# Attention: first scores of four heads as one block behind the output product, in other PSUM banks

## The chip, the cores and the metric

The kernel runs on one core of a Trainium2 chip. The time is device microseconds of one execution. TensorE (PE) multiplies into PSUM, eight banks of 128 partitions by 512 fp32; VectorE (DVE) and ScalarE (ACT) read PSUM and work element by element; GpSimd (POOL) does so on SBUF only; SyncE (SP) issues DMAs. Each engine runs its own list of instructions in order and waits for the others by semaphores.

## What is computed

A stream of 4096 tokens (16 sequences of 256) with 256 features passes six layers: experts, attention, experts, a feed-forward with looked-up weights, a recurrent layer, and the same feed-forward again. The change is in the attention, which has 16 heads and 64 memory slots a head. Its reference, cut:

```python
def _chunk_abc(q, k, v, s):
    z = cumlogsumexp(s, axis=2)
    g = exp(concatenate([z[:, :, :1], z[:, :, :-1]], axis=2) - z)
    p = exp(s - z)
    def step_k(hk, x):                       # over time
        hk = hk * g_t[:, :, None, :] + k_t[..., None] * p_t[:, :, None, :]
        return (hk, einsum('bhk,bhkm->bhm', q_t, hk))
    pvT = softmax(okT, axis=-1)
    def step_v(hv, x):
        hv = hv * g_t[..., None] + p_t[..., None] * v_t[:, :, None, :]
        return (hv, einsum('bhm,bhmv->bhv', pv_t, hv))
s = clip(x @ Ws, -32, 32)
o = o * rsqrt(mean(square(o)) + EPS) * g_norm_weight
o = o * (g * sigmoid(g))
x = x + o.reshape(b, t, VALUE_DIM) @ Wo
```

## The kernel before

The stages run one behind the other, each in a block of its own; attention is one. It treats the recurrences as two causal products. With e = exp(clipped s), the first scores of a head are k against q over the 64 key features, masked so that only earlier times count; they are then applied to e (the slots' read), divided by the running sum of e, and put through a softmax over the 64 slots. The second scores are e turned against those weights over the 64 slots, masked likewise, and applied to v (the value read). Then come the norm, the gate and the output product.

A group is four heads of one sequence: N = 64 groups in order, index n, four to a sequence. Each of the 64 rounds of the loop works on the group n (slots' read, softmax, second scores, value read), on the group n + 1 (its projections and first scores) and on the group n - 1 (its turned output and output product). Every engine's order is written out by hand, and semaphores are counted by group.

PSUM is full: psA (two banks) takes the projections, psB (two banks) the scores, psC[0] turned and read things and the output product, psC[1] the turned exponentials and the turned read, psD (two banks) the value read of both time tiles and the turned output; psO names the two halves of psD.

A head's scores are two matmuls, 64 rows deep: times 0 to 127 against all 256, and times 128 to 255 against themselves, 384 columns in one bank (`causal_scores`, L1264). Even heads use partitions 0 to 63 of their operands, odd heads 64 to 127. In the trace each fp32 matmul leaves two records, and the projections and the output product are split into a high and a low part, three matmuls each (L1449 to L1451).

On TensorE a round ends: `over_j(n)` (the value read, L1323), `scores_a(n + 1)` for heads 0 and 1, `output(n - 1)` (L1344), `scores_a(n + 1)` for heads 2 and 3. The next begins with a value projection and the slots' read (L1294). Heads 2 and 3 of the first scores take the same psB banks as heads 0 and 1, so they wait for the masks of those (`at_ok`, L1280). The second scores (`scores_b`, L1283) use psB and both halves of psD.

On VectorE (L1142 on) the round ends: two gated outputs (L1109), masks of heads 0 and 1 (L1096), two gates (L1103), the output's addition `add_output(n - 1)` (L1083), masks of heads 2 and 3, and `squares(n)` (L1122). ScalarE squares the value read and takes the tanh of the gates. GpSimd turns the mean squares into a scale (L966) and scales the output (L971). In one period of four the next sequence is turned too (L1198).

Of the kernel before, what the change touches and what calls it, by code (L numbers as in the profile page):

```python
# [801 lines left out]
def attention(nc, cst, w, tag, past, stream_a, stream_b, x_out, second, zero_row, indices, looked_up):  # L802
# [10 lines left out]
    with ExitStack() as ctx:  # L813
# [38 lines left out]
        psO = [psD[:, k, :] for k in range(2)]  # L852

# [21 lines left out]
        with nc.Block(no_gpsimd_drain=True) as block:  # L875
# [180 lines left out]
            def _(dve):  # L1056
# [39 lines left out]
                def masked(n, heads, ps_ready, done, late=psB):  # L1096
                    for h in heads:
                        dve.wait_ge(ps_ready, HQ * n + h + 1)
                        bank = psB[h] if h < 2 else late[h - 2]
                        nc.vector.tensor_tensor(out=at[:, h, :], in0=bank[:, 0:3 * P],  # L1100
                                                in1=cst["causal"][:, :, :].rearrange("p a i -> p (a i)"), op=ALU.mult).then_inc(done, 1)
# [36 lines left out]
                masked(0, (0, 1), at_ps, at_ok)  # L1138
                gate(0, 0)
                gate(0, 1)  # L1140
                masked(0, (2, 3), at_ps, at_ok)
                for n in range(N):  # L1142
# [25 lines left out]
                    masked(n, range(HQ), bt_ps, bt_ok, psO)  # L1168
# [13 lines left out]
                    if ahead:  # L1182
                        masked(n + 1, (0, 1), at_ps, at_ok)
# [4 lines left out]
                    if ahead:  # L1188
                        masked(n + 1, (2, 3), at_ps, at_ok)
# [5 lines left out]
            def _(pe):  # L1195
# [68 lines left out]
                def causal_scores(lhs, rhs, h, ready, late=psB):  # L1264

                    a, r = h // 2, (h % 2) * DK
                    bank = psB[h] if h < 2 else late[h - 2]
# [4 lines left out]
                def scores_a(m, heads):  # L1272
                    for h in heads:
                        if h < 2:
                            if m > 0:
                                pe.wait_ge(bt_ok, HQ * m - 1 + h)
                            pe.wait_ge(k_ok, m + 1)
                            pe.wait_ge(q_ok, m + 1)
                        else:
                            pe.wait_ge(at_ok, HQ * m + h - 1)  # L1280
                        causal_scores(kT, qT, h, at_ps)

                def scores_b(n):  # L1283

                    pe.wait_ge(pzt_ok, n + 1)
                    pe.wait_ge(et_ok, n + 1)
                    for h in range(HQ):
                        if h < 2:
                            pe.wait_ge(at_ok, HQ * n + h + 3)
                        elif n > 0:  # L1290
                            pe.wait_ge(otl_ok, NH * n)
                        causal_scores(emT, pzT, h, bt_ps, psO)
# [68 lines left out]
                scores_a(0, (0, 1))  # L1361
                gate(0, 1)
                scores_a(0, (2, 3))
                for n in range(N):
# [24 lines left out]
                    if ahead:  # L1389
                        scores_a(n + 1, (0, 1))  # L1390
# [678 lines left out]
```

## Time and profile before

| | us |
|---|---|
| median of 3 runs | 2752.42 |
| lowest, highest | 2749.83, 2756.99 |
| the profiled execution | 2760.54 |
| its span | 2758.7 |
| PE, DVE, ACT, POOL busy in it | 2413.2, 1805.3, 864.9, 1245.1 |

The rows below come from the profiled execution, in us from the start of its span; the rest of its 2760.54 us lies around the span. The granted clock of TensorE is given as a share: 1.00 is 2.4 GHz, half of it 1.2 GHz. Matmuls are pipelined: a matmul's length in a row covers the start of the next, so the rate is to be read from the distance of the starts. In names, a_ stands for the attention stage; a_at holds masked scores.

### The profile page before, as it was taken

Reading aid. Unit: us, or ns where it says so; the run is one execution under the profiler, and the core shown is the slowest. Engines: PE = TensorE matmul, PEld = TensorE weight load, DVE = VectorE, ACT = ScalarE, POOL = GpSimd, SP = SyncE. Lnnn points to the kernel's source line nnn. Section 1 sums busy time; section 2 is a strip of 40 time slices with the busy share of each in tenths; the row PEclk is TensorE's granted clock in tenths of the full one; section 3 lists DMA queues with packets and bytes.
Section 4 is the critical chain, followed back from the end, with each engine's and each line's share of the span. In section 5 each row is a group of like instructions: output and inputs, shape, how many; then the busy total and the mean of one; then the engine's idle time right before and its main releaser. Section 6 shows DMA issues by size and latency. Waiting matters only on the chain. (4 is left out here: it accounts for less than half of the span.)

```text
span 2758.7 us, 44491 instructions
## 1 busy us (share of the span) xinstructions
PE 2413.2 (87%) x16926; PEld 2123.4 (77%) x16926; DVE 1805.3 (65%) x3578; ACT 864.9 (31%) x1704; POOL 1245.1 (45%) x1214
## 2 busy tenths in 40 slices
PE   6555579999999999999999999996566588999997
PEld 5444468888888888888888888885555467888886
DVE  5422357888888888888887888775422257676654
ACT  4322223333333333333333333323322122333332
POOL 3277735554555455545554555452277622222110
PEclk9988889999999999999999999995598789999999
DMA  6798810000000000000000000004599710000000
GB/s 205 236 226 217 187 27 5 17 20 20 5 17 20 20 5 16 20 9 16 17 20 5 20 17 20 5 11 125 145 246 213 152 39 24 24 24 24 16 8 16
DMA packets 196930, 169.52 MB, mean 61 GB/s; under 512 B 28944, under 2 KB 189680, under 8 KB 196208
## 3 DMA queue, kind: packets, MB, share of 16 engines
q1 hardware_dynamic: 167040, 118.69, 14.6%
q0 software_dynamic: 24576, 37.77, 7.4%
q10 hardware_dynamic: 5104, 10.22, 1.2%
q8 instruction: 137, 2.24, 0.3%
q14 instruction: 73, 0.60, 0.1%
HBM read 117.94 MB, written 53.13 MB: 62 GB/s over the span
## 5 line engine op out<-in xcount | busy, mean ns | idle before, releaser
L966 POOL TENSOR_TENSOR a_orstd<-a_ms,minus_half 128x8 f32<-128x8 f32 x64 | 106.8, 1669 | 497.2 <-DVE a_ms L1127 496.0
L946 POOL TENSOR_SCALAR a_pick<-a_index,lut_row 128x258 f32<-128x258 int32 x240 | 280.7, 1170 | 24.3
L1100 DVE TENSOR_TENSOR a_at<-a_psB,causal 128x384 f32<-128x384 f32 x384 | 195.5, 551 | 58.6 <-PE a_psB L1269 58.6
L1120 DVE RECIPROCAL a_rz<-a_rz 128x256 f32<-128x256 f32 x128 | 215.6, 1715 | 0.0
L652 PE MATMUL e_psX<-ident,e_xg 128*128 128x128 f32 x256 | 63.9, 338 | 171.9 <-DMA e_xg<-rows,slot_tok 171.4
L776 DVE TENSOR_TENSOR e_hT<-e_psH,e_sil 128x128 f32<-128x128 f32 x128 | 37.3, 291 | 260.4 <-ACT e_sil L733 178.7
L652 PEld LDWEIGHTS e_psX<-ident,e_xg 128*128 128x128 f32 x256 | 32.6, 163 | 218.7 <-DMA e_xg<-rows,slot_tok 214.6
L1331 PEld LDWEIGHTS a_psD<-a_v,a_at 128*128 128x128 f32 x1536 | 181.3, 192 | 7.1 <-issue 1.4
L949 POOL TENSOR_TENSOR a_found<-a_found,a_pick 128x258 f32<-128x258 f32 x240 | 177.4, 739 | 20.0
L1331 PE MATMUL a_psD<-a_v,a_at 128*128 128x128 f32 x1536 | 181.8, 275 | 1.2 <-DVE a_at L1100 1.2
L622 POOL DMA_INDIRECT e_xg<-rows,slot_tok x128 | 129.8, 1014 | 109.4 <-POOLq L247 66.3
L977 ACT ACTIVATE a_v<-a_psA 128x512 f32<-128x512 f32 x128 | 76.5, 598 | 275.8 <-PE a_psA L1451 275.8
L1449 PE MATMUL a_psC<-wo_high,a_oT 128*128 128x256 f32 x512 | 151.9, 297 | 1.5 <-DVE a_oT L1079 1.5
L1449 PE MATMUL f_pair<-f_lnT,wguT 128*128 128x512 f32 (+1 forms) x352 | 143.6, 408 | 7.5 <-DVE f_lnT L1715 7.2
L1450 PE MATMUL a_psC<-wo_low,a_oT 128*128 128x256 f32 x512 | 144.5, 282 | 0.0
L1451 PE MATMUL a_psC<-wo_high,a_oT 128*128 128x256 f32 x512 | 144.5, 282 | 0.0
L1726 DVE TENSOR_TENSOR f_hs<-f_pair,f_sil 128x512 f32<-128x512 f32 x96 | 66.1, 689 | 117.0 <-PE f_pair L1451 106.8
L1450 PE MATMUL f_pair<-f_lnT,wguT 128*128 128x512 f32 (+1 forms) x352 | 140.9, 400 | 0.0
L1451 PE MATMUL f_pair<-f_lnT,wguT 128*128 128x512 f32 (+1 forms) x352 | 140.8, 400 | 0.0
L971 POOL TENSOR_TENSOR a_o<-a_o,a_orstd 128x512 f32<-128x512 f32 x128 | 131.2, 1046 | 5.0
L1049 ACT ACTIVATE a_sq<-a_psD 128x512 f32<-128x512 f32 x128 | 76.5, 598 | 177.3 <-PE a_psD L1331 165.8
L717 ACT ACTIVATE e_xgT<-e_psX 128x256 f32<-128x256 f32 x128 | 49.1, 384 | 243.2 <-PE e_psX L652 199.2
(252 smaller groups left out, 7572.3 us busy)
## 6 DMA issues: line engine op xcount, KB each, us to landing
e_wg<-in_L_ffn_w_gate SPq DMA_DIRECT2D x128, 128.0 KB
e_wu<-in_L_ffn_w_up SPq DMA_DIRECT2D x128, 128.0 KB
e_wd<-in_L_ffn_w_down SPq DMA_DIRECT2D x128, 128.0 KB
rows<-r_row SPq DMA_DIRECT2D x32, 320.0 KB, 3.2
stream_b<-r_zeros SPq DMA_DIRECT2D x11, 384.0 KB, 5.8
stream_c<-rows SPq DMA_DIRECT2D x33, 128.0 KB, 3.3
r_xt<-in_L_attn_hidden_states SPq DMA_DIRECT2D x16, 256.0 KB, 3.9
stream_a<-r_xt SPq DMA_DIRECT2D x16, 256.0 KB, 5.4
```

Of the source, the lines that this page charges most:

```text
L622: pool.indirect_dma_start(out=xg[:, e % U, :], out_offset=None, in_=rows, in_offset=bass.IndirectOffsetOnAxis(ap=slot_tok[:, e:e + 1], axi ...
L652: nc.tensor.transpose(psX[u][:, c, :], xg[:, e % U, c * P:(c + 1) * P], cst["ident"][:, :]).then_inc(turned[u], 1)
L946: nc.gpsimd.tensor_scalar(pick[:, :, :], index[:, :, :], float(c), w["lut"][:, c:c + 1], ALU.is_equal, ALU.mult).then_inc(picked, 1)
L949: nc.gpsimd.tensor_tensor(out=found[:, :, :], in0=found[:, :, :], in1=pick[:, :, :], op=ALU.add).then_inc(looked, 1)
L966: nc.gpsimd.tensor_tensor(out=flat(orstd[:, :, :]), in0=ms[:, :], in1=cst["minus_half"][:, 0:TT * HQ], op=ALU.pow).then_inc(orstd_ok, 1)
L971: nc.gpsimd.tensor_tensor(out=part, in0=part, in1=orstd[:, :, 2 * a:2 * a + 2].unsqueeze(3).to_broadcast([P, TT, 2, DV]), op=ALU.mult).the ...
L1100: nc.vector.tensor_tensor(out=at[:, h, :], in0=bank[:, 0:3 * P], in1=cst["causal"][:, :, :].rearrange("p a i -> p (a i)"), op=ALU.mult).th ...
L1120: nc.vector.reciprocal(rz[:, a, :], rz[:, a, :]).then_inc(rz_ok, 1)
L1331: mm = nc.tensor.matmul(psD[:, t, h * DV:(h + 1) * DV], bt[:, h, i * P:(i + 1) * P], v[:, n % 2, j, h * DV:(h + 1) * DV], start=(j == 0), ...
L1449: nc.tensor.matmul(out, lhs[0], rhs[0], start=first, stop=False)
L1450: nc.tensor.matmul(out, lhs[0], rhs[1], start=False, stop=False)
L1451: return nc.tensor.matmul(out, lhs[1], rhs[0], start=False, stop=last)
```

## The change

All four heads of the first scores are now issued in one block behind the output product. Heads 0 and 1 take the psB banks, head 2 takes psC[1] (the bank of the turned exponentials), head 3 the first half of psD (a bank of the second scores' and of the value read). The waits follow the banks: the block waits for the exponentials' copy and the masks of the second scores, head 3 also for the gated output and the squares of the group before. On VectorE the four masks follow each other behind the output's addition. The second scores keep their banks, and their waits are gathered.

```diff
--- before.py
+++ after.py
@@ -850,6 +850,8 @@
         psC = [mem.ps(f"psC{k}", [P, 512]) for k in range(2)]
         psD = mem.ps("psD", [P, 2, 512])
         psO = [psD[:, k, :] for k in range(2)]
+        first_banks = psB + [psC[1], psO[0]]
+        second_banks = psB + psO
 
         names = ("x_here x_out_done xs_ok xacc_ok stats moments shifted rstd_ok ln_ok ln_ps lnTh_ok lnTl_ok "
                  "v_ps v_ok q_ps q_ok k_ps k_ok g_ps th_ok tg_ok s_ps sc_ok em_ok scan_ok rz_ok et_ps et_ok "
@@ -1093,11 +1095,10 @@
                     dve.wait_ge(s_ps, m + 1)
                     nc.vector.tensor_scalar(flat(em[:, :, :]), psA[1 - m % 2], -32.0, 32.0, ALU.max, ALU.min).then_inc(sc_ok, 1)
 
-                def masked(n, heads, ps_ready, done, late=psB):
-                    for h in heads:
+                def masked(n, ps_ready, done, banks):
+                    for h in range(HQ):
                         dve.wait_ge(ps_ready, HQ * n + h + 1)
-                        bank = psB[h] if h < 2 else late[h - 2]
-                        nc.vector.tensor_tensor(out=at[:, h, :], in0=bank[:, 0:3 * P],
+                        nc.vector.tensor_tensor(out=at[:, h, :], in0=banks[h][:, 0:3 * P],
                                                 in1=cst["causal"][:, :, :].rearrange("p a i -> p (a i)"), op=ALU.mult).then_inc(done, 1)
 
                 def gate(m, t):
@@ -1135,10 +1136,9 @@
                     running_sum(0, a)
                 for a in range(NH):
                     invert(0, a)
-                masked(0, (0, 1), at_ps, at_ok)
                 gate(0, 0)
                 gate(0, 1)
-                masked(0, (2, 3), at_ps, at_ok)
+                masked(0, at_ps, at_ok, first_banks)
                 for n in range(N):
                     b, q = divmod(n, QPB)
                     ahead = n + 1 < N
@@ -1165,7 +1165,7 @@
                     nc.vector.tensor_tensor(out=flat(pzT[:, :, :]), in0=psC[0], in1=flat(rz[:, :, :]), op=ALU.mult).then_inc(pzt_ok, 1)
                     if n > 0:
                         low_of_output(n - 1)
-                    masked(n, range(HQ), bt_ps, bt_ok, psO)
+                    masked(n, bt_ps, bt_ok, second_banks)
                     if ahead:
                         dve.wait_ge(pzt_ok, n + 1)
                         running_sum(n + 1, 0)
@@ -1180,13 +1180,12 @@
                     dve.wait_ge(sq_ok, TT * n + 1)
                     gated_output(n, 0)
                     if ahead:
-                        masked(n + 1, (0, 1), at_ps, at_ok)
                         gate(n + 1, 0)
                         gate(n + 1, 1)
                     if n > 0:
                         add_output(n - 1)
                     if ahead:
-                        masked(n + 1, (2, 3), at_ps, at_ok)
+                        masked(n + 1, at_ps, at_ok, first_banks)
                     squares(n)
                 low_of_output(N - 1)
                 add_output(N - 1)
@@ -1261,35 +1260,35 @@
                             mm = nc.tensor.transpose(psC[1][:, a * T + t * P:a * T + (t + 1) * P], em[:, t, a * P:(a + 1) * P], ident)
                     mm.then_inc(et_ps, 1)
 
-                def causal_scores(lhs, rhs, h, ready, late=psB):
+                def causal_scores(lhs, rhs, h, bank, ready):
 
                     a, r = h // 2, (h % 2) * DK
-                    bank = psB[h] if h < 2 else late[h - 2]
                     nc.tensor.matmul(bank[:, 0:2 * P], lhs[r:r + DK, a, 0:P], rhs[r:r + DK, a, 0:T], start=True, stop=True)
                     nc.tensor.matmul(bank[:, 2 * P:3 * P], lhs[r:r + DK, a, P:T], rhs[r:r + DK, a, P:T],
                                      start=True, stop=True).then_inc(ready, 1)
 
-                def scores_a(m, heads):
-                    for h in heads:
-                        if h < 2:
-                            if m > 0:
-                                pe.wait_ge(bt_ok, HQ * m - 1 + h)
-                            pe.wait_ge(k_ok, m + 1)
-                            pe.wait_ge(q_ok, m + 1)
-                        else:
-                            pe.wait_ge(at_ok, HQ * m + h - 1)
-                        causal_scores(kT, qT, h, at_ps)
+                def scores_a(m):
+
+                    pe.wait_ge(k_ok, m + 1)
+                    pe.wait_ge(q_ok, m + 1)
+                    pe.wait_ge(et_ok, m + 1)
+                    if m > 0:
+                        pe.wait_ge(bt_ok, HQ * (m - 1) + 2)
+                    for h in range(HQ):
+                        if h == 3 and m > 0:
+                            pe.wait_ge(o1_ok, TT * m)
+                            pe.wait_ge(sq_ok, TT * m)
+                        causal_scores(kT, qT, h, first_banks[h], at_ps)
 
                 def scores_b(n):
 
                     pe.wait_ge(pzt_ok, n + 1)
                     pe.wait_ge(et_ok, n + 1)
+                    pe.wait_ge(at_ok, HQ * n + 2)
                     for h in range(HQ):
-                        if h < 2:
-                            pe.wait_ge(at_ok, HQ * n + h + 3)
-                        elif n > 0:
+                        if h == 2 and n > 0:
                             pe.wait_ge(otl_ok, NH * n)
-                        causal_scores(emT, pzT, h, bt_ps, psO)
+                        causal_scores(emT, pzT, h, second_banks[h], bt_ps)
 
                 def slots_read(n):
 
@@ -1358,9 +1357,8 @@
                 key(0)
                 turn_exps(0)
                 gate(0, 0)
-                scores_a(0, (0, 1))
                 gate(0, 1)
-                scores_a(0, (2, 3))
+                scores_a(0)
                 for n in range(N):
                     ahead = n + 1 < N
                     if ahead:
@@ -1386,13 +1384,11 @@
                             turn_stream((n + 1) // QPB + 1)
                         gate(n + 1, 1)
                     over_j(n)
-                    if ahead:
-                        scores_a(n + 1, (0, 1))
                     if n > 0:
                         pe.wait_ge(lnTl_ok, min((n + 1) // QPB + (2 if (n + 1) % QPB == QPB - 1 else 1), B))
                         output(n - 1)
                     if ahead:
-                        scores_a(n + 1, (2, 3))
+                        scores_a(n + 1)
                 turn_output(N - 1)
                 pe.wait_ge(acc_ok, N - 1)
                 output(N - 1)
```

TensorE's list from the value read of a group to the next value projection. Before (L1331 value read, L1268 and L1269 scores, a_psC<-wo the output product, a_psA<-wv the value projection):

```order
L1331 MATMUL a_psD<-a_v,a_at 128x128 x11
L1268 MATMUL a_psB<-a_qT,a_kT 128x256 [waits a_q_ok,a_k_ok,a_bt_ok]
L1269 MATMUL a_psB<-a_qT,a_kT 128x128
L1268 MATMUL a_psB<-a_qT,a_kT 128x256 [waits a_q_ok,a_k_ok,a_bt_ok]
L1269 MATMUL a_psB<-a_qT,a_kT 128x128
L1449 MATMUL a_psC<-wo_high,a_oT 128x256 [waits r1_tabled,a_lnTl_ok]
...
L1268 MATMUL a_psB<-a_qT,a_kT 128x256 [waits a_at_ok]
L1269 MATMUL a_psB<-a_qT,a_kT 128x128
L1268 MATMUL a_psB<-a_qT,a_kT 128x256 [waits a_at_ok]
L1269 MATMUL a_psB<-a_qT,a_kT 128x128
L1449 MATMUL a_psA<-wv_high,a_lnT 128x512 [waits a_tg_ok,a_lnTl_ok]
```

The same place in the changed kernel, from the last matmuls of the output product on (the value read now stands straight before the product; L1266 and L1267 are the scores):

```order
L1447 MATMUL a_psC<-wo_high,a_oT 128x256
L1266 MATMUL a_psB<-a_qT,a_kT 128x256 [waits a_et_ok,a_bt_ok,a_q_ok,a_k_ok]
L1267 MATMUL a_psB<-a_qT,a_kT 128x128
L1266 MATMUL a_psB<-a_qT,a_kT 128x256
L1267 MATMUL a_psB<-a_qT,a_kT 128x128
L1266 MATMUL a_psC<-a_qT,a_kT 128x256
L1267 MATMUL a_psC<-a_qT,a_kT 128x128
L1266 MATMUL a_psD<-a_qT,a_kT 128x256 [waits a_sq_ok,a_o1_ok]
L1267 MATMUL a_psD<-a_qT,a_kT 128x128
L1445 MATMUL a_psA<-wv_high,a_lnT 128x512 [waits a_tg_ok,a_lnTl_ok]
```

The first pair has moved behind the output product, and the second pair has banks of its own.

VectorE's list from the gated outputs of a group to its sum of squares. Before (L1110 gated outputs, L1100 masks, L1106 gates, L1089 the addition, L1124 the squares' sum):

```order
L1110 TENSOR_TENSOR a_o<-a_psD,a_tg 128x512 [waits a_tg_ok,a_ov_ps]
L1110 TENSOR_TENSOR a_o<-a_psD,a_tg 128x512 [waits a_sq_ok]
L1100 TENSOR_TENSOR a_at<-a_psB,causal 128x384 [waits a_at_ps] x2
L1106 SCALAR_TENSOR_TENSOR a_tg<-a_tg,a_psA 128x512 [waits a_th_ok] x2
L1089 TENSOR_TENSOR a_xacc<-a_psC,a_xacc 128x512 [waits r1_filled,a_xacc_ok,r1_tokened]
L1100 TENSOR_TENSOR a_at<-a_psB,causal 128x384 [waits a_at_ps] x2
L1124 TENSOR_REDUCE a_ss<-a_sq 128x8 [waits a_sq_ok]
```

In the changed kernel (the same operations, a line or two further on):

```order
L1111 TENSOR_TENSOR a_o<-a_psD,a_tg 128x512 [waits a_tg_ok,a_ov_ps]
L1111 TENSOR_TENSOR a_o<-a_psD,a_tg 128x512 [waits a_sq_ok]
L1107 SCALAR_TENSOR_TENSOR a_tg<-a_tg,a_psA 128x512 [waits a_th_ok] x2
L1091 TENSOR_TENSOR a_xacc<-a_psC,a_xacc 128x512 [waits r1_filled,a_xacc_ok,r1_tokened]
L1101 TENSOR_TENSOR a_at<-a_psB,causal 128x384 [waits a_at_ps] x2
L1101 TENSOR_TENSOR a_at<-a_psC,causal 128x384 [waits a_at_ps]
L1101 TENSOR_TENSOR a_at<-a_psD,causal 128x384 [waits a_at_ps]
L1125 TENSOR_REDUCE a_ss<-a_sq 128x8 [waits a_sq_ok]
```

The first two masks have moved behind the gates and the addition. Names that begin with r1_ are semaphores of an earlier stage that share a number with one of the attention's.

## Rows read from the trace of the kernel before

**Rows 1.** Windows: us, busy time (instructions) per engine, granted clock, DMA share, GB/s
```profile
400.00:1100.00 700.00, 700.00 (x5565) 627.62 (x5566) 567.76 (x899) 230.51 (x399) 357.53 (x354) 1.00 0.05 14
```

**Rows 2.** Waits of TensorE from 400 to 1853: total us, times, longest
```profile
PE a_psC L1319 <- ACT a_sq L1034: 2.2, 1, 2.2
...
```

**Rows 3.** Timeline of TensorE: start, us, engine, line, operation, out<-in, times
```profile
1276.69 2.84 PE L1331 MATMUL a_psD<-a_v,a_at 128*128 128x128 f32 x24
...
1299.83 2.84 PE L1331 MATMUL a_psD<-a_v,a_at 128*128 128x128 f32 x24
...
1302.39 0.28 PE L1331 MATMUL a_psD<-a_v,a_at 128*128 128x128 f32 x1
1302.60 0.71 PE L1268 MATMUL a_psB<-a_qT,a_kT 64*128 64x256 f32 x4
...
1303.46 0.39 PE L1449 MATMUL a_psC<-wo_high,a_oT 128*128 128x256 f32 x1
1303.68 0.28 PE L1450 MATMUL a_psC<-wo_low,a_oT 128*128 128x256 f32 x1
...
1306.50 0.71 PE L1268 MATMUL a_psB<-a_qT,a_kT 64*128 64x256 f32 x4
...
1307.36 0.51 PE L1449 MATMUL a_psA<-wv_high,a_lnT 128*128 128x512 f32 x1
...
1308.96 1.53 PE L1303 MATMUL a_psC<-a_at,a_em 128*64 128x128 f32 x24
```

**Rows 4.** Timeline of TensorE, end of the stage: value read straight into output product
```profile
1858.39 0.28 PE L1331 MATMUL a_psD<-a_v,a_at 128*128 128x128 f32 x1
...
1858.62 0.28 PE L1450 MATMUL a_psC<-wo_low,a_oT 128*128 128x256 f32 x1
```

**Rows 5.** Timeline of TensorE, second scores of four heads and the next gate
```profile
1318.49 0.71 PE L1268 MATMUL a_psB<-a_pzT,a_emT 64*128 64x256 f32 x4
...
1319.25 0.70 PE L1268 MATMUL a_psD<-a_pzT,a_emT 64*128 64x256 f32 x4
...
1320.10 0.50 PE L1449 MATMUL a_psA<-wg_high,a_lnT 128*128 128x512 f32 x1
```

**Rows 6.** Timeline of VectorE and ScalarE beside rows 3; brackets: idle before, releaser
```profile
1302.70 1.32 DVE L1110 TENSOR_TENSOR a_o<-a_psD,a_tg 128x512 f32<-128x512 f32 x2
...
1304.06 1.09 ACT L1011 ACTIVATE a_tg<-a_psA 128x512 f32<-128x512 f32 x2
...
1304.87 1.27 DVE L1106 SCALAR_TENSOR_TENSOR a_tg<-a_tg,a_psA 128x512 f32<-128x512 f32 x2
...
1306.61 0.69 DVE L1089 TENSOR_TENSOR a_xacc<-a_psC,a_xacc 128x512 f32<-128x512 f32 x1 [0.47 <-PE a_psC L1451]
...
1307.46 1.02 DVE L1100 TENSOR_TENSOR a_at<-a_psB,causal 128x384 f32<-128x384 f32 x2 [0.16 <-PE a_psB L1269]
```

**Rows 7.** Timeline of VectorE, four masks of the second scores
```profile
1319.44 1.02 DVE L1100 TENSOR_TENSOR a_at<-a_psB,causal 128x384 f32<-128x384 f32 x2 [0.79 <-PE a_psB L1269]
1320.38 1.01 DVE L1100 TENSOR_TENSOR a_at<-a_psD,causal 128x384 f32<-128x384 f32 x2
```

**Rows 8.** Timeline of VectorE in a period with a turned stream: gated outputs
```profile
1279.85 1.22 DVE L1110 TENSOR_TENSOR a_o<-a_psD,a_tg 128x512 f32<-128x512 f32 x2
```

**Rows 9.** Timeline of GpSimd's scaling and TensorE's turning of its result
```profile
1311.63 2.05 POOL L971 TENSOR_TENSOR a_o<-a_o,a_orstd 128x512 f32<-128x512 f32 x2
...
1316.09 1.04 PE L1340 MATMUL a_psD<-ident,a_o 128*128 128x128 f32 x8
```

**Rows 10.** Timeline ahead of the loop and of the last group with scores ahead
```profile
373.57 3.34 DVE L1120 RECIPROCAL a_rz<-a_rz 128x256 f32<-128x256 f32 x2
...
377.38 0.94 PE L1268 MATMUL a_psB<-a_qT,a_kT 64*128 64x256 f32 x3 [1.17 <-DVE a_at L1100]
...
378.69 0.50 PE L1449 MATMUL a_psA<-wv_high,a_lnT 128*128 128x512 f32 x1
...
1843.93 0.88 PE L1303 MATMUL a_psC<-a_at,a_em 128*64 128x128 f32 x12 [0.29 <-DVE a_at L1100]
```

## The prediction

> **What bounds the kernel now.** I read the page for the busy shares, then the waits of TensorE, then TensorE's timeline of one attention period, last VectorE and ScalarE at the same place. In the attention stage TensorE is busy without a break: 700.00 us of 700 at a granted clock of 1.00, its upper level of 2.4 GHz [rows 1]. Between 400 and 1853 us it waits for others four times in all, the longest 2.2 us [rows 2]. So the stage lasts as long as TensorE's instructions take to follow one another, and the busy share hides what matters: the distance from one start to the next. A period (one group of four heads) is 23.14 us, from the value read's start at 1276.69 to the next at 1299.83 [rows 3]. There are 64. No engine has to be relieved; what can be won is start-to-start time on TensorE, and what can be lost is a wait that TensorE does not have now.
>
> At the place of the change [rows 3] the last matmul of the value read starts at 1302.39, the first pair of scores at 1302.60, the output product at 1303.46 with its second matmul at 1303.68, the second pair of scores at 1306.50, the next value projection at 1307.36, the slots' read at 1308.96. A pair of heads costs 0.86 us to the next start each time. The output product's matmuls otherwise follow each other at 0.12: 24 of them fill 1303.46 to 1306.50, 3.04 us, of which the first takes 0.22.
>
> **The change on TensorE.** The same matmuls are issued; two are written to other banks. Three junctions change.
>
> (a) Value read to output product, now adjacent. Before: 1302.39 to 1303.68, 1.29 us from the last value read to the output's second matmul [rows 3]. The neighbourhood exists once in the trace, at the end of the stage, where no scores stand between: 1858.39 to 1858.62, 0.23 us [rows 4]. That is 1.06 less, of which 0.86 only moves on; 0.20 is gained. I count to the second matmul because the first output matmul after the scores is followed late.
>
> (b) The rest of the output product and its passage into 64-row scores stay: 1303.68 to 1306.50, 2.82 us.
>
> (c) Four heads in one block. The second scores already run so, in the two psB banks and the two psD banks, from 1318.49 to the following gate's 1320.10: 1.61 us [rows 5]. Two separate pairs cost 2 x 0.86 = 1.72. 0.11 is gained.
>
> From the last value read to the next value projection: before 1307.36 - 1302.39 = 4.97 us; after 0.23 + 2.82 + 1.61 = 4.66. 0.31 us a period. By the rows it is the passage between 128-row and 64-row matmuls that is paid twice too often: 0.21 instead of 0.11 (value read to scores), 0.20 at the way out, 0.22 for the first output matmul. The Trainium skill (TensorEngine Tiling, Key Properties) says the same in kind: a change of tiling mode drains TensorE, a change of tile within a mode does not. Counting only the excess of the two drains, about 0.09 each by those rows, this rule alone would give 0.18 us a period and about 11 us in all; I take the direct rows of (a) and (c), which hold the late first output matmul too.
>
> The waits attached to these matmuls go from eight to six. A first or second head with three satisfied waits starts 0.01 us beside its partner in the rows of before (the two first starts lie inside the x4 row at 1302.60), so satisfied waits cost nothing. The new ones are satisfied: the turned exponentials' copy is over before the value read ends, and the gated output and the squares have left psD by 1304.02 [rows 6], 2.5 us before the new head 3 wants its bank.
>
> **The change on VectorE, and who waits for it.** Set the value read's start to 0 (1299.83). The masks of heads 0 and 1 used to run under the output product; now all four stand behind the output's addition. What is queued behind them: the sum of squares, then the normalised read; who waits: the slots' read on TensorE for the masks, GpSimd for the squares.
> - Gated outputs end at 4.19 as before. The gates need the tanh of ScalarE, 4.23 to 5.32 [rows 6]: the first can start at about 4.83, and two take 1.27, ending at 6.15.
> - The addition needs the output product. It now ends 1.06 us earlier: the addition's release moves from 6.78 [rows 6] to 5.72. So VectorE, at 6.13, does not wait for it any more; the addition ends near 6.82.
> - TensorE starts the scores at 0.23 + 2.56 + 2.82 = 5.61. The first mask can run at once, four in a row take 1.95 (1319.44 to 1321.39 [rows 7]): 6.75 to 8.70. Before, the last mask ended at 1308.48, which is 8.65.
> - The slots' read starts at 5.61 + 1.61 + 1.60 = 8.82 (1.60 is the value projection, 1307.36 to 1308.96). It needs heads 0 and 1, done at 7.7, and for its second half heads 2 and 3, half of its 1.46 us later, at 9.55. Spare: 1.1 and 0.85 us.
> - In the 15 periods with a turned stream VectorE begins its gated outputs at 3.16 (1279.85 against 1276.69 [rows 3, 8]) instead of 2.87: 0.29 of the spare goes, 0.55 stays.
> - The squares come 0.05 later against the value read and 0.36 later against TensorE's next step. GpSimd ends the first of its two scalings near 1312.7 and TensorE turns it from 1316.09 on [rows 9]: 3.4 us of spare hide that.
>
> So no new wait in a regular period. It is 61 periods (group 1 to 61): 61 x 0.31 = 18.9 us. The last one with scores ahead has no value projection as cover and already waits 0.29 us for the masks [rows 10]; they end 0.05 later there, so it gains nothing. Around the first group, where no output product lies between the pairs, the single pair of banks makes TensorE wait (1.17 us at 377.38 [rows 10]). Ahead of the loop the gates now come before the masks: the inversions end at 376.91 [rows 10], two gates take 1.2, four masks 1.95, so the masks end at 380.05 and the slots' read 0.73 later, near 380.8, instead of 378.69 + 1.60 + 1.46 = 381.75: 0.9 gained. For the scores of group 1, which stand behind the value read of group 0 with nothing between, a like sum gives 0.3. Total 18.9 + 0.9 + 0.3 = 20.1 us.
>
> **Against which time.** The profiled execution took 2760.54 us, of which the span is 2758.7; less 20.1 that is 2740.4. The median of the other runs is 2752.42 (2749.83 to 2756.99). The profile lies 8 above it; I subtract from the median: 2732.3 us, 0.73% less. What follows the attention stage starts when its last output is added, so the gain is not taken back by a transfer: the DMA share in the stage is 0.05 [rows 1].
>
> **Rivals.**
> 1. The second pair of the new block loses its overlap (ends slower). Heads 2 and 3 share the array only if both may start; head 3 alone waits for the squares and the gated output. How it looks when the pair is pulled apart is in the trace: a pair of first scores late by a wait takes 377.38 to 378.69, 1.31 us instead of 0.86 [rows 10]. With the first pair's 0.76 (1318.49 to 1319.25) the block would cost 2.07 instead of 1.61, a period 0.15 more than before, 62 x 0.15 = 9 us slower: about 2760 by the median (with 1 us back from the first groups). It decides when the wait is satisfied less than some tenths before; by [rows 6] it is satisfied 2.5 us before. 4%.
> 2. The masks become what the slots' read waits for: the gain is eaten. It needs VectorE 0.85 us later than summed (0.55 in 15 periods). An addition that still waited 0.25 and masks waiting for each score would be 0.4 late: not enough. From 1.16 us on, all 0.31 is gone and the time is as before, 2751 to 2753. For it: four masks and the addition now lie in one chain behind the output. Against it: TensorE's own steps lie in the same chain and are longer. 8%.
> 3. The drains cost, but the late first output matmul stays and the new block is no shorter than two pairs: 0.1 to 0.2 a period, 6 to 12 us and 1 at the start: 2739 to 2745. The bounds of (a) are 0.10 (only the value read's last step shrinks) and 0.20, of (c) 0 and 0.11. 15%.
> 4. The change does as summed: 2727 to 2738 with the spread of the runs. 73%.
>
> **How the numbers follow.** The likeliest is 4: 2732.3. The range reaches from 2727 (the runs before spread 3 to 4 us about their median) to 2742, which takes in most of rival 3; outside stand rivals 1 and 2 and a rest of 3. A measurement of this kernel can tell about 0.3%, 8 us, from no change: faster by more is case 4 and about three quarters of case 3, 0.85 with a little off for the runs' drift; within 0.3% is rival 2 and the rest of 3, 0.12; slower is rival 1's upper half, 0.03.
>
> **What would show it.** Profile after: value read's last matmul to the output's second 0.23; four first scores in 1.61 to the value projection; value read to value read 22.83 instead of 23.14; the slots' read without idle time before it but for the first two groups and the last; VectorE's addition without a wait, four masks in 1.95. Wrong if the block takes over 1.7, if the slots' read shows waits for the masks, or if periods are shorter by 0.31 but the total does not fall.

## The result, and the profile after

The changed kernel takes 2728.82 us (median of 4 runs, 2726.78 to 2733.78) against 2751.12 us before (4 runs, 2747.26 to 2756.99): ratio 0.9917, 95% interval 0.9896 to 0.9939. That is 0.83% less by the ratio; the forecast was 2732.3, and its range of 2727 to 2742 holds the median. Run once more (e8) it took 2730.38 against 2751.80, ratio 0.9933 [0.9915, 0.9951].

The profiled execution took 2733.78 us with a span of 2731.9, against 2760.54 and 2758.7 before. The engines' busy shares, from the page:

```profile
PE 2390.3 (87%) x16926; PEld 2116.9 (77%) x16926; DVE 1798.4 (66%) x3578; ACT 865.1 (32%) x1704; POOL 1244.1 (46%) x1214
```

The same stretch as [rows 1]: TensorE is still busy in all 700 us, at the same granted clock of 1.00, its level of 2.4 GHz, but it gets 5629 matmuls done in them where it did 5565. The busy share cannot show a gain that lies in the distance between starts; the count can.

```profile
400.00:1100.00 700.00, 700.00 (x5629) 635.28 (x5628) 571.28 (x911) 234.91 (x406) 367.48 (x364) 1.00 0.05 14
```

TensorE's waits from 400 to 1830 us (engine, tile and line that wait, then engine, tile and line waited for: total us, times, longest). As in [rows 2] there is nothing that repeats with the period; the third is the slots' read in the last group that has scores ahead:

```profile
PE a_psC L1318 <- ACT a_sq L1036: 2.2, 1, 2.2
PE a_psC L1311 <- DVE a_sq L1147: 1.1, 1, 1.1
PE a_psC L1302 <- DVE a_at L1101: 0.5, 1, 0.5
```

TensorE's timeline at the place of the change, the counterpart of [rows 3] (L1330 value read, L1445 to L1447 products with the split weights, L1266 scores, L1302 slots' read):

```profile
1306.32 2.84 PE L1330 MATMUL a_psD<-a_v,a_at 128*128 128x128 f32 x24
...
1308.92 0.37 PE L1445 MATMUL a_psC<-wo_high,a_oT 128*128 128x256 f32 x1
1309.12 0.28 PE L1446 MATMUL a_psC<-wo_low,a_oT 128*128 128x256 f32 x1
...
1311.94 0.71 PE L1266 MATMUL a_psB<-a_qT,a_kT 64*128 64x256 f32 x4
...
1312.70 0.38 PE L1266 MATMUL a_psC<-a_qT,a_kT 64*128 64x256 f32 x1
1312.71 0.47 PE L1266 MATMUL a_psD<-a_qT,a_kT 64*128 64x256 f32 x1
...
1313.55 0.49 PE L1445 MATMUL a_psA<-wv_high,a_lnT 128*128 128x512 f32 x1
...
1315.15 1.53 PE L1302 MATMUL a_psC<-a_at,a_em 128*64 128x128 f32 x24
...
1329.19 2.84 PE L1330 MATMUL a_psD<-a_v,a_at 128*128 128x128 f32 x24
```

Read by starts: the last value read stands at 1308.89, so value read to the output's second matmul is 0.23; the rest of the output product 1309.12 to 1311.94, 2.82; the four heads 1311.94 to 1313.55, 1.61. Heads 2 and 3, in their two new banks, start 0.01 us apart, so the second pair has its overlap. The value projection then takes 1.60 to the slots' read. Value read to value read is 22.87 us here; the four kinds of period are 22.86, 22.87, 22.87 and 23.30, where they were 23.13, 23.18, 23.18 and 23.61.

VectorE's timeline beside it (last column: shapes; in brackets the idle time before and who ended it), the counterpart of [rows 6]:

```profile
1309.20 1.32 DVE L1111 TENSOR_TENSOR a_o<-a_psD,a_tg 128x512 f32<-128x512 f32 x2
1311.19 1.28 DVE L1107 SCALAR_TENSOR_TENSOR a_tg<-a_tg,a_psA 128x512 f32<-128x512 f32 x2 [0.66 <-ACT a_tg L1013]
1312.39 0.68 DVE L1091 TENSOR_TENSOR a_xacc<-a_psC,a_xacc 128x512 f32<-128x512 f32 x1
1312.99 1.01 DVE L1101 TENSOR_TENSOR a_at<-a_psB,causal 128x384 f32<-128x384 f32 x2
1313.92 0.54 DVE L1101 TENSOR_TENSOR a_at<-a_psC,causal 128x384 f32<-128x384 f32 x1
1314.39 0.54 DVE L1101 TENSOR_TENSOR a_at<-a_psD,causal 128x384 f32<-128x384 f32 x1
```

The addition does not wait any more (0.47 us in [rows 6]): VectorE's own queue now ends last there. The four masks run from 6.67 to 8.61 us after the value read's start, and the slots' read starts at 8.83.

### The profile page after: what moved, and what is told of

The parts are those of the page before. It is cut to its first block and busy times, and to the rows that moved or that the text cites. A ratio compares the mean times of both kernels' runs of the same rounds, so it can differ in the third digit from the quotient of the medians.

```text
span 2731.9 us, 44553 instructions
## 1 busy us (share of the span) xinstructions
PE 2390.3 (87%) x16926; PEld 2116.9 (77%) x16926; DVE 1798.4 (66%) x3578; ACT 865.1 (32%) x1704; POOL 1244.1 (46%) x1214
## 5 line engine op out<-in xcount | busy, mean ns | idle before, releaser
L948 POOL TENSOR_SCALAR a_pick<-a_index,lut_row 128x258 f32<-128x258 int32 x240 | 281.4, 1172 | 24.3
L1330 PEld LDWEIGHTS a_psD<-a_v,a_at 128*128 128x128 f32 x1536 | 181.3, 192 | 7.2 <-issue 1.5
L1330 PE MATMUL a_psD<-a_v,a_at 128*128 128x128 f32 x1536 | 181.8, 275 | 1.2 <-DVE a_at L1101 1.2
L1101 DVE TENSOR_TENSOR a_at<-a_psB,causal 128x384 f32<-128x384 f32 x256 | 130.2, 550 | 48.8 <-PE a_psB L1267 48.8
L1445 PE MATMUL a_psC<-wo_high,a_oT 128*128 128x256 f32 x512 | 150.5, 294 | 1.5 <-DVE a_oT L1081 1.5
L1445 PE MATMUL f_pair<-f_lnT,wguT 128*128 128x512 f32 (+1 forms) x352 | 143.7, 408 | 7.5 <-DVE f_lnT L1711 7.2
L1447 PE MATMUL a_psC<-wo_high,a_oT 128*128 128x256 f32 x512 | 144.7, 283 | 0.0
L1447 PE MATMUL f_pair<-f_lnT,wguT 128*128 128x512 f32 (+1 forms) x352 | 140.7, 400 | 0.0
```

The source lines that it names most:

```text
L948: nc.gpsimd.tensor_scalar(pick[:, :, :], index[:, :, :], float(c), w["lut"][:, c:c + 1], ALU.is_equal, ALU.mult).then_inc(picked, 1)
L1101: nc.vector.tensor_tensor(out=at[:, h, :], in0=banks[h][:, 0:3 * P], in1=cst["causal"][:, :, :].rearrange("p a i -> p (a i)"), op=ALU.mult ...
L1330: mm = nc.tensor.matmul(psD[:, t, h * DV:(h + 1) * DV], bt[:, h, i * P:(i + 1) * P], v[:, n % 2, j, h * DV:(h + 1) * DV], start=(j == 0), ...
L1445: nc.tensor.matmul(out, lhs[0], rhs[0], start=first, stop=False)
L1447: return nc.tensor.matmul(out, lhs[1], rhs[0], start=False, stop=last)
```

## The experiments

Each was compared with the kernel before on the same chip. All edits are against the changed kernel.

**Is it the order or the banks?** e1 keeps the new banks and puts both engines back to the old order.

```
+scores_a(n + 1, (0, 1))      # before the output product, as it was
 if n > 0: output(n - 1)
-scores_a(n + 1)
+scores_a(n + 1, (2, 3))      # VectorE: masks (0, 1) before the gates, (2, 3) after the addition
```

> The new banks and waits of the changed kernel, in the order of before on TensorE and VectorE (heads 0 and 1 ahead of the output product and of the gates, heads 2 and 3 behind). Theory (TensorE pays for passages between 128-row and 64-row matmuls, and the order takes one round trip away): nothing is gained, value read to value read stays 23.18 us in a plain period, median 2751. Rival (the gain comes from the banks: heads 2 and 3 no longer wait for the masks of heads 0 and 1): period 22.87, median 2729.

Measured: 2752.61 us (10 runs) against 2753.11, ratio 0.9998 [0.9981, 1.0015]. The value read's starts in its TensorE timeline:

```profile
1292.22 2.84 PE L1333 MATMUL a_psD<-a_v,a_at 128*128 128x128 f32 x24
...
1315.40 0.50 PE L1333 MATMUL a_psD<-a_v,a_at 128*128 128x128 f32 x3
```

23.18 us, the period of the old order. Other banks for heads 2 and 3 are worth nothing alone in the repeating periods. (In the first one, where heads 2 and 3 used to wait for masks, they bring 0.17: 21.50 instead of 21.67.)

**What do they make possible?** e2 keeps the new order, but all four heads share the two psB banks, so that heads 2 and 3 wait for the masks of heads 0 and 1.

```
-first_banks = psB + [psC[1], psO[0]]
+first_banks = psB + psB
...
-if h == 3 and m > 0:
-    pe.wait_ge(o1_ok, TT * m)
-    pe.wait_ge(sq_ok, TT * m)
+if h >= 2:
+    pe.wait_ge(at_ok, HQ * m + h - 1)
...
-pe.wait_ge(at_ok, HQ * n + 2)    # second scores
+pe.wait_ge(at_ok, HQ * n + 4)
```

> The order of the changed kernel, but the two psB banks for all four first scores, so that heads 2 and 3 wait for the masks of heads 0 and 1. Theory: the masks now stand behind the output's addition and the first ends 7.3 us after the value read's start, while heads 2 and 3 are due at 6.4; they start late and pulled apart, the next value projection 1.3 to 1.5 us late: period 24.2 to 24.4, median 2810 to 2820. So the banks are what lets the order be had. Rival (banks do not matter): 22.87, 2729.

Measured: 2822.53 us (2 runs) against 2753.02, ratio 1.0249 [1.0206, 1.0293], slightly above the 2810 to 2820 expected. TensorE's timeline of the block:

```profile
1342.67 0.71 PE L1266 MATMUL a_psB<-a_qT,a_kT 64*128 64x256 f32 x4
...
1344.32 0.94 PE L1266 MATMUL a_psB<-a_qT,a_kT 64*128 64x256 f32 x3 [0.72 <-DVE a_at L1101]
...
1345.63 0.50 PE L1444 MATMUL a_psA<-wv_high,a_lnT 128*128 128x512 f32 x1
```

Heads 2 and 3 start 1.65 us after heads 0 and 1 instead of 0.76, and the pair, pulled apart, takes 1.31 instead of 0.85. The block costs 2.96 instead of 1.61, and the period is 24.22, longer by just that 1.35. So the order alone loses 2.5%, and the banks are what lets it gain.

**Is VectorE's new order needed?** e3 has the new order on TensorE and the old one on VectorE: masks of heads 0 and 1 before the gates, the others after the addition.

> TensorE as in the changed kernel, VectorE in the order of before: masks of heads 0 and 1 ahead of the gates. Theory: VectorE waits for the scores until 6.6 us after the value read's start, the first gate ends near 8.2, and the next value projection, due at 7.2, waits for that gate to free its bank: 1.0 us a period, 23.9, median 2785 to 2795. Rival (VectorE's order does not matter as it has spare): 22.87, 2729.

Measured: 2804.38 us (2 runs) against 2753.02, ratio 1.0183 [1.0154, 1.0213]. Its row in TensorE's waits:

```profile
PE a_psA L1447 <- DVE a_tg L1107: 60.2, 58, 1.0
```

VectorE stands before the masks until the scores come, the gates stand behind the masks, and the value projection behind the gates, 1.0 us in each of 58 periods. The period was 23.96 as expected (23.9); the total was some 10 to 20 us above the median expected. Most of that lies in the expectation itself: 61 periods that are 0.78 longer (23.96 instead of 23.18) are already 48 us, about 2800. Another 5 us are seven periods that begin with the value read of a sequence's first group and took 24.04 to 26.27. The output's addition ends at 9.39 there, where the changed kernel has it at 6.75; e6 shows what hangs on it.

**What does one passage between tile sizes cost?** e4 puts half of the next value projection (three 128-row matmuls) between heads 0, 1 and heads 2, 3. The same matmuls run, with one more passage to 128 rows and back.

```
 for h in range(HQ):
+    if h == 2 and m + 1 < N: value_half(m + 1, 0)
     causal_scores(kT, qT, h, first_banks[h], at_ps)
...
-value(n + 1, 0)
+value_half(n + 1, 1)
```

> The changed kernel, but the first half of the next value projection (3 of 6 matmuls) stands between heads 0,1 and heads 2,3: one more passage into and out of 64-row matmuls, no matmul more. Theory: the block's saving of 0.11 is lost, the second pair is entered 0.09 later and the second half of the projection begins 0.11 late, 0.31 us a period together: 23.18 again, median 2748 to 2751. Rival (the gain is that the output product follows the value read, whatever comes later): about 22.9 to 22.98, median 2729 to 2736. Masks of heads 2 and 3 end some 0.5 us later, within the spare.

Measured: 2748.93 us against 2753.11, ratio 0.9983 [0.9967, 0.9998]. TensorE's timeline:

```profile
1283.97 0.71 PE L1273 MATMUL a_psB<-a_qT,a_kT 64*128 64x256 f32 x4
...
1284.83 0.49 PE L1454 MATMUL a_psA<-wv_high,a_lnT 128*128 128x512 f32 x1
...
1285.73 0.48 PE L1273 MATMUL a_psC<-a_qT,a_kT 64*128 64x256 f32 x1
...
1286.59 0.51 PE L1454 MATMUL a_psA<-wv_high,a_lnT 128*128 128x512 f32 x1
...
1287.48 1.53 PE L1311 MATMUL a_psC<-a_at,a_em 128*64 128x128 f32 x24
```

Scores and value projection together take 1283.97 to 1287.48, 3.51 us, against 1.61 + 1.60 = 3.21 in the changed kernel. One more round trip costs 0.30 in these rows and 0.32 in the period, which is back at 23.19. TensorE has no wait in these periods. (The total is 0.17% under that of before, with an interval that just leaves out no change. The two traces do not show where: the attention stage took 1520.67 us in e4's and 1519.82 in that of before. The cause of these 4 us stays open.) That is the gain of the change seen by its opposite: the passage is the price, here between halves of a value projection, in e1 on both sides of the output product. The Trainium skill (TensorEngine Tiling, Key Properties), on which the prediction draws, has a change of tiling mode drain TensorE. In kind the trace agrees; but the two drains alone, 0.18 by the rows of the prediction, are less than what is measured. The rest is the first 128-row matmul after scores, which is followed late: at the output product by 0.22 instead of 0.12, [rows 3], and at the value projection by 0.33 instead of 0.24. The changed kernel pays that last one once a period, e4 twice. No run puts other matmuls of 64 rows in the scores' place, so that it is the number of rows, and not something else in how the scores are issued, is argued from the rows and the page and not shown by itself.

**How much spare do the masks have?** e5 lets VectorE sum the squares ahead of the four masks.

```
+squares(n)
 if ahead:
     masked(n + 1, at_ps, at_ok, first_banks)
-squares(n)
```

> The changed kernel, but on VectorE the sum of squares and the small operation behind it (1.41 us together) stand ahead of the four masks instead of behind: a measured delay for the masks. By the spare summed for them (1.1 us for heads 0 and 1, 0.85 for heads 2 and 3), the slots' read waits about 0.3 us at its start and its second half begins 0.5 to 0.6 us late: period 23.4, median 2760 to 2766. Rival (more spare than summed, VectorE does not bind): 22.87, 2729. Rival (no spare at all, rival 2 of the prediction): 1.4 a period, 2815.

Measured: 2765.92 us (10 runs) against 2753.11, ratio 1.0052 [1.0035, 1.0069]. First its row in TensorE's waits, then its timeline of TensorE:

```profile
PE a_psC L1302 <- DVE a_at L1101: 18.4, 59, 0.5
```

```profile
1301.27 2.84 PE L1330 MATMUL a_psD<-a_v,a_at 128*128 128x128 f32 x24
...
1310.43 1.71 PE L1302 MATMUL a_psC<-a_at,a_em 128*64 128x128 f32 x24 [0.27 <-DVE a_at L1101]
```

The last mask ends 9.94 us after the value read's start instead of 8.61, 1.33 later, and the period is 23.38, 0.51 longer. So 0.82 of the delay cost nothing: the prediction's spare of 0.85 for heads 2 and 3. In the 15 periods for which it had 0.55, the period goes from 22.86 to 23.56, which leaves a spare of 0.63. This is rival 2 built for the test, and the delay from which it decides is where the prediction put it.

**Can the block stand elsewhere?** e6 puts it between the two halves of the output product, which has the same number of passages, with VectorE's masks ahead of the addition, since the output is now finished later.

```
-output(n - 1)
+output(n - 1, (0,))
 if ahead: scores_a(n + 1)
+if n > 0: output(n - 1, (1,))
...
+if ahead: masked(n + 1, at_ps, at_ok, first_banks)    # VectorE
 if n > 0: add_output(n - 1)
-if ahead: masked(n + 1, at_ps, at_ok, first_banks)
```

> The changed kernel, but the block of four heads stands between the two halves of the output product (time tile 0 ahead, time tile 1 behind), and the masks run ahead of the addition. The number of passages into and out of 64-row matmuls is as in the changed kernel. Theory: only their number counts, period 22.87, median 2729. Rival (what was gained is the neighbourhood of the block and the value projection): 22.95 to 23.1, median 2734 to 2743.

Measured: 2743.56 us (10 runs, 2728.27 to 2750.64) against 2753.11, ratio 0.9959 [0.9939, 0.9979]: faster than before, but by about half of what was expected. The median lies beside that of the expectation's rival, the periods do not: most are within 0.03 us of the changed kernel's. But the period that begins with the value read of a sequence's first group takes 23.07 to 25.18, in 14 of 15 cases (after the last one there is no next sequence), and the 61 periods last 1410.03 us instead of 1401.29. (The traced execution took 2736.45, 7 us less than the median; the others may have lost more there.) One such place, by engine (TensorE; the value read before started at 844.33):

```profile
862.68 0.71 PE L1266 MATMUL a_psB<-a_pzT,a_emT 64*128 64x256 f32 x4
...
863.67 0.71 PE L1266 MATMUL a_psD<-a_pzT,a_emT 64*128 64x256 f32 x4
```

```profile
855.17 0.61 POOL L934 COPY a_xacc<-a_xab 128x512 f32<-128x512 f32 x1 [12.49 <-DMA x_att<-a_xacc]
855.74 1.67 POOL L968 TENSOR_TENSOR a_orstd<-a_ms,minus_half 128x8 f32<-128x8 f32 x1
857.49 2.04 POOL L973 TENSOR_TENSOR a_o<-a_o,a_orstd 128x512 f32<-128x512 f32 x2
859.49 1.28 POOL L922 TENSOR_TENSOR a_xab<-a_xab 128x512 f32<-128x512 f32 x1
```

```profile
860.08 0.72 DVE L1158 SCALAR_TENSOR_TENSOR a_es<-a_sm 128x8 f32<-128x8 f32 x1
860.81 0.75 DVE L1062 BATCH_NORM_STATS2 a_bs<-a_xab 128x6 f32<-128x256 f32 x2
...
861.76 0.66 DVE L1165 TENSOR_TENSOR a_pzT<-a_psC,a_rz 128x512 f32<-128x512 f32 x1
862.34 1.28 DVE L1081 TENSOR_TENSOR a_oT<-a_psD,a_oT 128x512 fp32r<-128x512 f32 x2
```

The addition ends 8.61 us after the value read's start instead of 6.75. In this period it completes the last sequence's attention output, which is stored; GpSimd's copy into the same buffer waits for that store, and starts at 10.84 instead of 8.98. The normalising scale stands behind the copy, the next sequence's addition (L922) behind the scale, VectorE's moments of that sequence (L1062) behind this addition, the softmax weights (L1165) behind the moments, and behind these the low part of the turned output (L1081). It ends at 863.62, and only then is the bank free in which the second pair of scores starts at 863.67: 0.99 after the first pair, not 0.76, which is the 0.23 that this period of 23.10 is too long. In a plain period there is no store and no copy, and the chain has slack. The load of the next sequence, which L922 adds, also waits for the copy. In the five longest of the 14 periods something came on top: the store took 2.62 to 4.28 us from the addition's end to the copy instead of 2.22 (23.48, 24.80 and 25.18) or 2.42 (23.29), or the load came late (23.83).

**Is it this chain?** e7 is e6 with the addition ahead of head 3's mask, 0.4 us earlier, and nothing else.

```
+masked(n + 1, at_ps, at_ok, first_banks, (0, 1, 2))
 if n > 0: add_output(n - 1)
+masked(n + 1, at_ps, at_ok, first_banks, (3,))
```

> The kernel with the block between the halves of the output product, but with the addition ahead of the mask of head 3 instead of behind it, so that it ends about 0.47 us earlier (8.15 instead of 8.61 us after the value read's start). Question: why did the first group of each sequence take 23.1 us and more there, while all other groups took 22.87 as forecast. Theory: the store of the finished sequence waits for the addition, GpSimd's copy waits for the store, behind it stand GpSimd's scaling and the sum of the next stream, VectorE waits for that sum ahead of the softmax weights, and the second scores on TensorE wait for those; the chain is 0.2 us too late there. With 0.47 us given back most of these groups return to 22.87, those with a slow store excepted; median 2732 to 2738 against 2743.6. Rival (the halves around the block cost something of themselves in that group): 23.1 as before, 2743.

Measured: 2736.26 us (7 runs) against 2750.67, ratio 0.9959 [0.9941, 0.9976]. In its trace 8 of the 14 long periods are back at 22.87 or 22.88. The six others take 23.03 to 24.34: in four the store took 2.55 to 3.74, in the other two (23.03 and 23.98) it took its 2.22 and L922 waited for the next sequence's load. The 61 periods last 1404.95. The same period as above (value reads at 838.09 and 860.96, 22.87):

```profile
848.54 0.62 POOL L934 COPY a_xacc<-a_xab 128x512 f32<-128x512 f32 x1 [12.01 <-DMA x_att<-a_xacc]
...
852.86 1.28 POOL L922 TENSOR_TENSOR a_xab<-a_xab 128x512 f32<-128x512 f32 x1
```

And the period of 23.98, with the load late:

```profile
761.15 1.27 POOL L922 TENSOR_TENSOR a_xab<-a_xab 128x512 f32<-128x512 f32 x1 [1.24 <-DMA a_xab<-stream_b]
```

The copy starts at 10.45, 0.39 earlier than in e6, and the period's excess is gone. Where store and load take their usual time, the halves around the block thus cost nothing of themselves, and the chain through the copy is what e6 paid for. The 61 periods are 5.1 us shorter than e6's, but that is not all the work of the 0.4 us: 1.9 of it is one period whose store took 3.81 in e6 and 2.26 in e7. The totals do not tell the two kernels apart: both ratios are 0.9959, and the traced execution of e7, 2724.60 us, was the fastest of its seven. What made single stores and loads slow stays open.

**How far does the size of the gain repeat?** e8 is the changed kernel once more.

> The changed kernel itself, with more runs beside runs of before on one chip, to tell the sum of the prediction (20.1 us, of which the two traces show 19.2 in the attention stage) from the 22.3 between the two medians so far. If the attention stage holds the whole gain: ratio 0.9930 and a difference of 19 to 20 us. If something outside it gains too: 0.9919 or less, 22 us or more.

Measured: 2730.38 us (6 runs, 2727.53 to 2739.58) against 2751.80 (11 runs), ratio 0.9933 [0.9915, 0.9951], 18.4 us by the ratio and 21.4 between the medians. The interval holds both of its expectations; it does not tell them apart. In its trace the 61 periods last 1401.29 us, the same to 0.01 as in the other trace of the changed kernel.

## Why the prediction was right, point by point

**The bound.** TensorE's start-to-start time set the stage, and still does. Every experiment that changed the distance of two starts without a new wait (e1, e4, e6's plain periods) moved the period by that distance to within 0.02, and nothing else made up for it.

**Term (a), 0.20.** Predicted 0.23 from the last value read to the output's second matmul, measured 0.23, where before it was 1.29 with 0.86 of scores in it. **Term (b), 0.** 2.82 against 2.82. **Term (c), 0.11.** 1.61 against 1.61. The neighbourhoods did exist in the trace of before, in another place [rows 4, 5], and reading them there was exact to 0.01 us. Forecasting from the excess of the two drains alone, 0.18, would have missed 0.13: e4 measures 0.30 for a round trip, and the change gives 0.31.

**The sum.** Predicted 61 x 0.31 = 18.9 us. By the starts of the value reads of groups 1 and 62, the rows that stand first and last in the two TensorE timelines, it is 1420.10 us before and 1401.29 after, 18.81 less:

```profile
415.12 1.05 PE L1331 MATMUL a_psD<-a_v,a_at 128*128 128x128 f32 x8
...
1835.22 2.84 PE L1331 MATMUL a_psD<-a_v,a_at 128*128 128x128 f32 x24
```

```profile
410.24 1.95 PE L1330 MATMUL a_psD<-a_v,a_at 128*128 128x128 f32 x16
...
1811.53 1.72 PE L1330 MATMUL a_psD<-a_v,a_at 128*128 128x128 f32 x14
```

The single period was predicted as 22.83 from one of 23.14. That kind, which begins with the value read of a sequence's third group, is 22.86 now, 0.27 shorter; the other kinds are 0.31 shorter. And 0.3 of the 18.81 is an accident of the trace of before: a store of 3.81 us made its period 23.54 where its like took 23.18. Without it the 61 periods gave 18.5, so the 0.31 of the sum is right in three kinds of period of four, and that the two traces come within 0.1 of the sum is in part luck.

**The ends of the loop.** First group: 0.3 predicted, 21.67 to 21.45 = 0.22 measured. Ahead of the loop: from the end of the inversions to the slots' projection, before 376.91 to 381.75, after 373.24 to 377.09:

```profile
369.90 3.34 DVE L1121 RECIPROCAL a_rz<-a_rz 128x256 f32<-128x256 f32 x2
```

```profile
373.92 0.47 PE L1445 MATMUL a_psA<-wv_high,a_lnT 128*128 128x512 f32 x1 [0.84 <-DVE a_tg L1107]
...
377.09 0.39 PE L1445 MATMUL a_psA<-ws_high,a_lnT 128*128 128x256 f32 x1
```

4.84 to 3.85, 0.99 gained where 0.9 was predicted. One thing was not seen: the value projection there now waits 0.84 us for the first gate, which stands behind the inversions on VectorE. The prediction's sum went by VectorE's queue, which ends last there, so the wait cost nothing; it replaced the wait for the masks of [rows 10]. Of this gain the stage as a whole shows less, since its first part, which the change does not touch, happened to be longer in that trace: from the stage's start to the first value read it is 37.23 before and 36.87 after. The last period was 20.53 and is 20.51, no gain as said; but that it comes out so exactly is luck. In it TensorE waits for others, and its granted clock can fall. These are the last second scores, first in this trace (4.30 us, granted clock 0.61), then in that of e8, the same kernel (3.60 us, 0.98), where the last period is 19.78 and not 20.51:

```profile
1827.70:1832.00 4.30, 3.15 (x17) 2.41 (x16) 3.33 (x6) 0.60 (x1) 3.93 (x5) 0.61 0.00 0
```

```profile
1824.60:1828.20 3.60, 1.92 (x17) 1.43 (x16) 3.25 (x6) 0.60 (x1) 3.33 (x4) 0.98 0.00 0
```

The clock of this stretch is in no term of the prediction.

**From the stage to the total.** The stage, from its first GpSimd addition to its last addition on VectorE, went from 1519.8 to 1500.6 us: 19.2 of the 20.1 predicted (in e8's trace it is 1500.0, 19.8 less). The spans differ by 26.8. The other 7.6 lie before the stage (356.2 to 351.9) and after it (882.7 to 879.4), where no instruction changed; they are the spread between two executions. Subtracting from the median, and not from the longer profiled execution, was the right choice: 2752.42 - 20.1 = 2732.3 against 2728.82 and 2730.38. The medians differ by 22.3 and 21.4, the stage by 19.2 and 19.8; whether something outside it gains too stays open, e8 included.

**VectorE and GpSimd.** Gates' end predicted at 6.15, measured 6.15; addition from 6.13 to 6.82, measured 6.07 to 6.75; masks 6.75 to 8.70, measured 6.67 to 8.61; slots' read 8.82, measured 8.83. The spare of 0.85 behind head 3's mask is 0.82 by e5. GpSimd's scaling had 3.4 us of spare by the sum, and 3.16 in this trace.

**The rivals.** 1 (the second pair loses its overlap) did not come: heads 2 and 3 start 0.01 apart. What it would have cost shows in e2, whose pulled-apart pair takes 1.31 us, the figure taken from [rows 10]. 2 (the masks eat the gain) did not come, and e5 shows that it takes 0.82 us of delay to begin. 3 (only a part of it) is excluded by terms (a) and (c). A rival that was not named is the one of e6: the output's addition comes later, and through the store, GpSimd's copy and the next sequence's addition it makes 14 periods longer. The prediction's list of who waits for VectorE leaves this chain out. In the change the addition came at 6.75 where it had ended at 7.47 before, so the chain was given slack and not put under strain: the trace of before has one period that a slow store made 0.36 longer, e1's has one of 24.01 with a store of 4.29 us, and the two traces of the changed kernel, whose slowest store took 2.53, have none.

## What to carry to other kernels

Where an engine is busy without a break, its busy time says nothing about what can be won; read the distances from one start to the next, and look in the same trace for a place where the new neighbours already stand side by side. On TensorE each round trip from 128-row tiles to 64-row tiles and back cost about 0.3 us here, so scores of several heads belong in one block, but only with a bank for each head: with shared banks the same order lost 2.5%. When an operation moves later, follow it to the end even where it looks free, above all through a store whose buffer is filled anew.

## What was not expected of the hardware

In e6 the small VectorE operation of L1158, on 8 columns, took 0.72 us, and in e7 the same one 0.34; an operation of its size and kind takes 0.17 (L1128 in e5). In both it ended 0.03 us behind the end of GpSimd's addition L922: in e6 at 860.80 beside 860.77, in e7 at 854.17 beside 854.14 (L922 is shown above for both):

```profile
853.83 0.34 DVE L1158 SCALAR_TENSOR_TENSOR a_es<-a_sm 128x8 f32<-128x8 f32 x1
854.18 0.43 DVE L1062 BATCH_NORM_STATS2 a_bs<-a_xab 128x6 f32<-128x256 f32 x1
```

It reads two operands from SBUF, and looks held until GpSimd's instruction has ended. These are not two single cases: in the two traces a GpSimd TENSOR_TENSOR was under way 89 times when L1158 began (by over 0.05 us, and with over 0.05 us to go), and each time L1158 ended 0.02 to 0.03 us behind its end, after 0.17 to 1.10 us. The Trainium skill (SBUF — State Buffer, SBUF: two separate sides) says that a VectorE operation with two SBUF inputs and a GpSimd operation that reads SBUF exclude each other for a whole instruction; for TENSOR_TENSOR on GpSimd the rows agree, though no run was made to test it. For GpSimd's TENSOR_SCALAR (L948), which reads SBUF as well, they do not: it was running 34 times when L1158 began, and L1158 took 0.17 to 0.27 us and ended 0.19 to 0.68 us ahead of it. Here the measurement decides; why the two kinds differ is not shown. A duration from the trace of such a small operation can thus hold some of its neighbour's. It cost nothing of its own in the two rows shown, since the moments behind it waited for the same GpSimd addition.
